# Attention in a vision-transformer layer: the transposes of the probabilities issued ahead of the next tile's scores

## What is computed

```
q = _layernorm((x @ Wq.T).reshape(N, L, H, D).transpose(0, 2, 1, 3), gq, bq)
k = _layernorm((x @ Wk.T).reshape(N, L, H, D).transpose(0, 2, 1, 3), gk, bk)
scores = jnp.einsum('nhld,nhmd->nhlm', q, k)
scores = jnp.where(causal, scores, NEG)
attn = jax.nn.softmax(scores, axis=-1)
out = jnp.einsum('nhlm,nhmd->nhld', attn, v)
return out.transpose(0, 2, 1, 3).reshape(N, L, EMB) @ Wo.T + bo
```

## Time and profile before

| | us |
|---|---|
| median of 3 runs | 410.04 |
| lowest and highest | 409.7, 416.57 |
| the profiled execution | 411.02 |
| its span, first to last instruction | 409.2 |
| TensorE matmuls, busy | 350.8 (86%) |
| VectorE, busy | 219.0 (54%) |
| ScalarE, busy | 183.2 (45%) |
| GpSimd, busy | 151.8 (37%) |

### The profile page before, as it was taken

The page is one execution under the profiler, slowest core; times in us unless marked ns, Lnnn a source line. Parts: engine busy times, 40 slices in busy tenths (PEclk is TensorE's granted clock), DMA queues, the critical chain, the costliest instruction groups (busy, mean ns, idle before and its releaser), DMA issues.

```text
span 409.2 us, 7271 instructions
## 1 busy us (share of the span) xinstructions
PE 350.8 (86%) x2080; PEld 294.2 (72%) x2081; DVE 219.0 (54%) x582; ACT 183.2 (45%) x435; POOL 151.8 (37%) x176
## 2 busy tenths in 40 slices
PE   3998999598999999469896579978999999995795
PEld 2886555397888888237684478858999998994694
DVE  0227577879899998527899962351011101213175
ACT  1000454788888894048530013144555555441231
POOL 1002713224465564540140064025776676532000
PEclk9999999759999999658999989999999999999599
DMA  7641411231111100942102000035666666541342
GB/s 270 245 142 62 169 55 61 71 135 48 48 47 46 46 1 2 400 137 70 35 7 96 0 2 26 0 92 165 211 225 210 192 217 219 161 148 41 136 145 84
DMA packets 20537, 45.67 MB, mean 112 GB/s; under 512 B 2150, under 2 KB 12836, under 8 KB 20260
## 3 DMA queue, kind: packets, MB, share of 16 engines
q1 hardware_dynamic: 17732, 37.78, 28.2%
q0 software_dynamic: 2496, 6.82, 4.8%
q10 hardware_dynamic: 288, 0.81, 0.7%
HBM read 38.18 MB, written 7.22 MB: 111 GB/s over the span
## 4 chain that ended last, share of the span: by engine, by line
PE 55%; DVE 19%; issue 11%; DMA 6%; POOL 3%; DVEq 2%; ACT 1%; SPq 0%; ACTq 0%; POOLq 0%
PE banks L1165 6%; PE banks L1351 6%; PE banks L1430 5%; PE banks L1439 5%; PE banks L1195 4%; PE banks L1248 4%; PE banks L1272 4%; PE banks L1485 3%; DMA qn_sb<-z_rows,gidx_sb 3%; PE banks L1495 2%; PE banks L1235 2%; DVE qk_sb L1038 2%; PE banks L1200 2%; PE banks L1221 2%; PE banks L1290 2%
## 5 line engine op out<-in xcount | busy, mean ns | idle before, releaser
L1102 DVE TENSOR_TENSOR pT_sb<-banks,p_sb 128x256 f32<-128x256 f32 x26 | 11.0, 425 | 83.4 <-issue 49.4
L1430 PE MATMUL banks<-qn_sb,w_sb 128*128 128x128 f32 x416 | 50.8, 275 | 1.0 <-ACT qn_sb L674 1.0
L1430 PEld LDWEIGHTS banks<-qn_sb,w_sb 128*128 128x128 f32 x416 | 48.6, 192 | 1.3 <-ACT qn_sb L674 1.2
L1439 PE MATMUL banks<-w_sb,sq_sb 128*128 x208 | 49.0, 379 | 0.0
L1439 PEld LDWEIGHTS banks<-w_sb,sq_sb 128*128 128x128 f32 x208 | 37.6, 190 | 4.1
L489 POOL DMA_INDIRECT y_rows<-pT_sb,sidx_sb x26 | 25.8, 993 | 35.6 <-DVE pT_sb L1102 35.6
L685 ACT ACTIVATE sq_sb<-banks,col_sb 128x128 f32<-128x128 f32 x104 | 32.3, 364 | 14.1 <-PE banks L1430 13.4
L674 ACT ACTIVATE qn_sb<-banks,col_sb 128x128 f32<-128x128 f32 x52 | 21.0, 454 | 38.1 <-PE banks L1417 29.5
L1165 PE MATMUL banks<-wtok_sb,patch_sb 128*114 128x256 f32 x132 | 31.6, 406 | 6.9 <-DMA wtok_sb<-in_w_tok 6.9
L483 POOL DMA_INDIRECT qn_sb<-z_rows,gidx_sb x26 | 26.9, 1035 | 22.7 <-PE banks L1417 18.1
L1165 PEld LDWEIGHTS banks<-wtok_sb,patch_sb 128*114 128x114 f32 x132 | 25.3, 193 | 12.4 <-DMA patch_sb<-in_patches 6.5
(11 more groups left out here) (213 smaller groups left out, 685.9 us busy)
## 6 DMA issues: line engine op xcount, KB each, us to landing
w_sb<-in_w SPq DMA_DIRECT2D x26, 512.0 KB
w_sb<-in_w SPq DMA_DIRECT2D x1, 4096.0 KB, 12.6
patch_sb<-in_patches SPq DMA_DIRECT2D x11, 342.0 KB, 3.0
vrep_sb<-v_rows SPq DMA_DIRECT2D x33, 114.0 KB
qk_sb<-y_rows SPq DMA_DIRECT2D x10, 228.0 KB
v_rows<-v_sb SPq DMA_DIRECT2D x11, 114.0 KB
z_rows<-h_sb SPq DMA_DIRECT2D x11, 114.0 KB
out_rows<-h_sb SPq DMA_DIRECT2D x10, 114.0 KB
```

What stands on the lines that cost most here:

```text
L1430: last = nc.tensor.matmul(bank[2 + 2 * s + c // 2][:, (c % 2) * 128:(c % 2 + 1) * 128], w1_sb[:, w0:w0 + 128], xsT_sb[:, (2 * s + k) * 128 ...
L1439: last = nc.tensor.matmul(bank[6 + s][:, 0:D], hidT_sb[:, s * HID + k * 128:s * HID + (k + 1) * 128], w2_sb[:, ds(e * 4 * D + k * D, D)], ...
```

## The change

In TensorE's program for a step of the attention stage, `turn_probs(t)` moves from behind `scores(t + 1)` to ahead of it, with its waits:

```
@@ -1295,9 +1295,9 @@
                 if ahead(t, 2):
                     turn_q(t + 2, s)
                     turn_k(t + 2, s)
+                turn_probs(t, s)
                 if ahead(t, 1):
                     scores(t + 1, 1 - s)
-                turn_probs(t, s)
                 if behind(t, 2):
                     output(t - 2, ahead(t, 2))
                 values(t, s)
```

## The result

The changed kernel takes 419.63 us (median of 4 runs, 416.98 to 427.78) against 409.87 for the kernel before in the same comparison. The ratio is 1.022 with a 95% interval of 1.0118 to 1.0321: slower, with 2% inside the interval, and the forecast of 1.4% too. The main mechanism of the forecast is there line for line. Single executions of either kernel differ by some per cent, with TensorE's granted clock: the ratios leave the slow ones out (here 427.78 of the changed kernel and 416.57 of the one before), and the three of the changed kernel that stay have a median of 417.27.

A forecast was written before the change was run, and what follows sets the result against it. VectorE's own work was taken to set the 7.42 us step. Seven steps at +0.82 gave +5.7, with steps 0, 1, 9 and 10 at zero: 410.04 + 5.7 = 415.7 us, range 412.8 to 419.0.

The forecast's parts named there:

- What bounds the kernel: Attention stage: VectorE's own work sets the 7.42 us step; TensorE stands still for 0.43 us before L1290.
- The seven steps: Attention steps 2 to 8, which hold the output block: 7.42 us each before, +0.82 each, 5.7 us in total.
- The wait: Before L1259, TensorE stops 1.26 us for ScalarE's query copy (L555) in every step with t up to 8.
- the ninth place: Sign of being right: 1.2 to 1.4 us of idle time before L1259, ended by L555, in nine places.
- The step: TensorE from one L1221 to the next: 8.18 to 8.30 us, taken as 8.24, +0.82 a step.
- Its spare time: VectorE in the new step has some 0.4 us to spare, expected as 0.4 to 0.6 idle before L863.
- Steps 9 and 10: Last attention steps, with no new queries: nothing to wait for, order inside them free, zero change.
- Steps 0 and 1: First attention steps, without output: step 0 about even, step 1 +0.15; together zero, between -0.5 and +1.0 us.
- Hidden copy: Rival: ScalarE's query copy is done in time or the stop is only apparent; time 410.0 us; chance 0.04.
- Sequencer losing its lead: Rival: behind the stop, waits of scores, output and values are paid openly; step 8.89, total 420.3 us; chance 0.09.
- The clock: Rival: TensorE's clock falls to half in some step, +6.2 us for each; one gives 421.9 us; chance 0.05.

The follow-up runs named there:

- mid: Kernel before with the new order (probability transposes ahead of the scores) in steps 2 to 8 alone; median 415.37 us, ratio 1.0162.
- step0: Kernel before with the new order (probability transposes ahead of the scores) in step 0 alone; ratio 1.0065, median 417.31 us.
- edge: Kernel before with the new order (probability transposes ahead of the scores) in steps 0, 1 and 9 alone; ratio 1.0029.
- after_slice: Changed kernel with the last of ScalarE's three query copies made in two halves; ratio 1.0354.
- not0: Changed kernel with the old order kept in step 0, the new order everywhere else; ratio 1.016.
- before_fill: Kernel before with eleven matmuls whose results nobody reads put into TensorE's two long idle times ahead of step 0; ratio 1.0092.
- split scores: Kernel before with the probability transposes moved between the two halves of the scores; ratio 0.9979.

## Why the prediction was right, and where it was not

- What bounds the kernel. The seven steps of 7.42 and the stop of 0.43 were read rightly, and a change on TensorE alone could indeed not gain there. "VectorE's own work sets the 7.42" was half of it: with 0.9 us of work taken from it the step shrank by 0.13 only, since a second loop was nearly as long.
- The wait. `q_kept` behind ScalarE's copy: expected 1.26 us of stop, measured 1.18 to 1.32 in steps 1 to 8. In step 0, the ninth place, it is 0.54. Its terms: L555 1.07 behind L1221 (the same), 1.82 (the same), hand-over 0.10, measured 0.15, the other end of the bound. That the copy and nothing else is what costs is shown by the two kernels that lengthen it and the one that shortens it.
- The step. 8.24 expected, 8.26 measured: 3.04 to L1259, 0.61, 1.80, 0.89 for the output block, 1.68, 0.25. The seven steps gave +5.8 against 5.7, and mid's 415.37 stands beside the predicted 415.7. The change as a whole came out above that: the median of all four executions, 419.63, is 0.6 beyond the upper end of the stated range (419.0), and the 417.27 of the result is inside it. In the profile 6.2 us were lost where 5.7 were forecast, and that they are so close is in part luck: -0.4 in steps 0 and 1, +1.2 behind the stage and an earlier start by 0.4 nearly cancel.
- VectorE. Its spare time was right in size, but I put it before L863. It is before L875, for the first half of the scores: these come 0.6 us of transposes and 1.3 us of stop later.
- Steps 9 and 10: neutral, as worked out. From the start of step 9 to the probability transposes of step 10 it is 5.21 us (159.68 to 164.89); it was 5.18 (154.64 to 159.82).
- Steps 0 and 1. Put at zero together, and the trace of the change gives -0.4. Step 1 is 7.36 us, as the 7.38 of the prediction has it. Step 0 gained 0.5, and not for the reason given there: the clock rose to 1.00 at 90.0 instead of 91.2, so its scores took 1.79 us instead of 2.35. This is the weak term of the prediction, because I counted step 0 at a fixed clock. Its stop of 0.5 us falls where TensorE still works at 1.2 GHz, and with the new order in step 0 alone most executions are 3 us or more above the median of the kernel before. The range of -0.5 to +1.0 for these two steps is too narrow for that: in the profile of step0 steps 0 to 2 lose over 9 us.
- The rivals. Hidden copy: excluded by the trace. Sequencer losing its lead: no; the blocks behind the stop stand at 0.61, 1.80, 0.89 and 1.68, against 0.59, 1.80, 0.86 and 1.68 without one. The clock: priced for a step in the middle, where it did not happen, and not looked for in step 0, where it did in edge, after_slice, step0 and not0.

I had weighed a rule of the Trainium skill against the trace ("TensorE: Matmul & The Clock Gate", A second HAM failure mode: psum-queue depth-cycling: many short idle times make the clock swing). The seven steps don't bear it out: the clock is 1.00 throughout. In the late rises, and behind the two stops of before_fill, the clock stayed low in one piece, for 20 to 34 us; a swing back and forth with the stops is in none of the traces.

No version here is measurably faster than the kernel before. The split scores are the best of the new orders that compute the whole, at 0.9979 with 1 inside the interval.

## What to carry to other kernels

Before moving a block forward in an engine's order, take its waits along and ask for each what covered it until now: here 1.8 us of scores lay over a copy of 1.8 us, and the move uncovered it in every step, while nothing about the work changed. Half of the cover was nearly enough, so a block can often be placed inside the work it would be exchanged with. And where an engine is as full as its neighbours, relieving one shows the next loop at once (7.42 to 7.29), so a bound is best tested by taking work away before one builds on it.

## What was not expected of the hardware

- Step 0 takes 7.9 us or 11.6 us, by when TensorE's granted clock rises from 0.50 to 1.00. With a stop of 0.5 us in it (step0) long executions are frequent, nine of eleven against two of 17; without it they occur too. TensorE can be busy nearly without a break, 23.75 of the 24.10 us from 90.6 to 114.7 in that trace, and still have 0.50.
- Keeping TensorE busy through 1.9 and 2.7 us of idle time held 2.4 GHz there, and behind two stops of 1.25 and 1.26 us within 3.3 us it was lost for 20 us; a single stop of 1.3 us every 8.3 us never lost it.
- Slicing one 32x304 copy of ScalarE (0.60 us) in two cost 0.23 us, less than the 0.34 that the duration of a 32x152 copy (0.47) suggested. The three whole copies take 1.82, no less than their durations together (3 x 0.60); with the last one halved it is 2.05, less than 2 x 0.60 + 2 x 0.46: the two halves overlap by nearly 0.1 us.
